# The first two stages of a bidirectional Mamba loop: convolution on VectorE, token tiles ahead of the loop, a new slot table

## What is computed

```
x   = patches @ W_tok.T                              # 16 tiles of 98 tokens
xz  = layernorm(x) @ W_in.T ; xc, z = split(xz)      # 384 + 384 channels
xconv = silu(conv_b + sum(conv_w[:, k] * xc[t + k - 3] for k in range(4)))
proj  = xconv @ W_x.T ; dtr, B, C = split(proj)      # 12, 16, 16
dt  = softplus(dtr @ W_dt.T + b_dt)
h[t] = exp(dt * A) * h[t-1] + (dt * xconv) * B       # 16 states per channel
y   = (sum_n h * C + xconv * D) * silu(z)
out += y @ W_out.T
```

## Time and profile before

| | us |
|---|---|
| median of three runs | 1530.7 |
| profiled execution, time / span | 1525.57 / 1523.8 |
| TensorE busy | 1337.1 (88%) |
| VectorE busy | 911.9 (60%) |
| ScalarE busy | 672.0 (44%) |
| GpSimd busy | 553.1 (36%) |
| granted TensorE clock, mean | 0.949 |

### The profile page before, as it was taken

How to read it: one execution, slowest core, us unless ns; L and a number is a source line. 1 busy time by engine, 2 the same in 40 slices (tenths; PEclk the granted TensorE clock), 3 DMA queues, 4 the chain that set the end, 5 groups by cost and what they waited for, 6 DMA issues and landing times.

```text
span 1523.8 us, 18483 instructions
## 1 busy us (share of the span) xinstructions
PE 1337.1 (88%) x6708; PEld 774.0 (51%) x6708; DVE 911.9 (60%) x1501; ACT 672.0 (44%) x1209; POOL 553.1 (36%) x399
## 2 busy tenths in 40 slices
PE   7888898898989877649988859989999899999998
PEld 6644454454545434326443345547856659445444
DVE  2487999999999999983100038865546624221122
ACT  4656777676767754232110106641542241313311
POOL 1266798989798887500000020012025302000000
PEclk9999899999999999869999969999999999999999
DMA  6504040504133240062999950000010000020101
GB/s 203 170 2 143 27 143 28 169 13 160 52 120 97 74 160 10 28 283 95 396 400 392 400 148 1 1 0 1 1 37 2 2 1 15 23 100 22 37 1 32
DMA packets 38773, 151.96 MB, mean 100 GB/s; under 512 B 10364, under 2 KB 14587, under 8 KB 33948
## 3 DMA queue, kind: packets, MB, share of 16 engines
q1 hardware_dynamic: 34588, 149.21, 27.7%
q10 hardware_dynamic: 4096, 1.58, 0.4%
HBM read 147.56 MB, written 1.63 MB: 98 GB/s over the span
## 4 chain that ended last, share of the span: by engine, by line
PE 54%; DVE 20%; issue 10%; ACT 6%; DMA 5%; POOL 3%; SPq 1%; ACTq 0%; DVEq 0%; POOLq 0%
PE ps L1854 53%; DVE arena L1452 7%; DVE arena L1441 4%; DMA arena<-in_e_b 4%; POOL arena L822 3%; ACT arena L924 2%; ACT ps L1035 1%; DVE stats L1372 1%; PE ps L1863 1%; DVE arena L1737 1%; ACT arena L929 1%; DVE arena L1461 1%; SPq L634 1%; DVE arena L1492 0%; DVE arena L1741 0%
## 5 line engine op out<-in xcount | busy, mean ns | idle before, releaser
L1854 PE MATMUL ps<-arena 128*98 128x192 f32 (+14 forms) x5260 | 954.7, 416 | 100.7 <-DVE arena L1502 25.1
L1854 PEld LDWEIGHTS ps<-arena 128*98 128x98 f32 (+12 forms) x5260 | 543.6, 154 | 483.3 <-issue 285.5
L822 POOL TENSOR_TENSOR arena<-arena 128x784 f32<-128x784 f32 x192 | 367.6, 1928 | 109.0 <-DVE arena L1452 108.4
L1854 PE MATMUL ps<-arena,ident 128*128 128x392 f32 x900 | 353.3, 523 | 48.4 <-POOL arena L822 40.2
L1452 DVE TENSOR_TENSOR_SCAN arena<-ps,arena 128x784 f32<-128x784 f32 x192 | 341.7, 1780 | 9.5 <-ACT ps L1035 9.5
L1854 PEld LDWEIGHTS ps<-arena,ident 128*128 128x128 f32 x900 | 172.0, 198 | 197.7 <-POOL arena L822 68.9
L924 ACT ACTIVATE arena<-ps 128x392 f32<-128x392 f32 (+9 forms) x265 | 124.3, 487 | 302.7 <-PE ps L1854 218.2
L1035 ACT ACTIVATE ps<-arena 128x384 f32<-128x384 f32 x384 | 207.8, 574 | 106.8 <-DVE arena L1452 106.2
L924 ACT ACTIVATE arena<-ps,arena 128x392 f32<-128x392 f32 (+2 forms) x194 | 105.1, 601 | 231.5 <-PE ps L1854 146.4
L1441 DVE TENSOR_TENSOR arena<-ps,arena 128x784 f32<-128x784 f32 x192 | 183.4, 956 | 12.6 <-issue 6.9
L1600 DVE COPY arena<-ps 128x384 f32<-128x384 f32 x32 | 16.4, 553 | 150.7 <-PE ps L2103 150.7
(11 more groups left out here) (199 smaller groups left out, 856.3 us busy)
## 6 DMA issues: line engine op xcount, KB each, us to landing
arena<-in_e_w SPq DMA_DIRECT2D x32, 2304.0 KB
arena<-bc_rows SPq DMA_DIRECT2D x128, 392.0 KB, 4.7
arena<-in_patches SPq DMA_DIRECT2D x4, 1176.0 KB, 7.7
arena<-comb_rows SPq DMA_DIRECT2D x1, 3136.0 KB, 10.7
arena<-in_mlp_w SPq DMA_DIRECT2D x5, 576.0 KB, 4.4
arena<-arena ACTq DMA_DIRECT2D x128, 12.0 KB, 8.5
arena<-in_mlp_w SPq DMA_DIRECT2D x5, 384.0 KB, 3.7
arena<-in_mlp_w SPq DMA_DIRECT2D x10, 192.0 KB, 4.0
```

Of the source, the lines that this page charges most:

```text
L822: pool.tensor_tensor(pair(hbuf[:, at % SLOTS, :]), pair(hbuf[:, at % SLOTS, :]), c_all[:, n:n + 2, :], ALU.mult).then_inc(times_c, 1)
L1854: return pe.matmul(dst, lhsT, rhs, start=first, stop=last)
```

## The change

The first stage's convolution leaves TensorE and its copies leave ScalarE: VectorE does it from the padded `xc` with one scale-and-bias and three multiply-adds per block (`first_conv`), interleaved with the silu products; the norm of tiles 4 to 7 moves behind them. `first_products` now counts nine steps, looked up by name in `FIRST_DONE`. All 16 token tiles use banks 0 to 5, are copied out ahead of the loop, and tiles 8 to 10 stand ahead of the first projection on TensorE. The second stage's preparation gets new slots: inner products in -3 to -1 (were 0 to 2), convolutions in 0 to 2 (were 4, 6, 8), projection 7 (11), steps 9 to 10 (12 to 13), du 20 (22); its z products take the usual slots. The third stage loses its exceptions. The late norm moves from slot 8 to 12 and its scalings from 10 to 14.

```diff
@@ -68,23 +68,22 @@
 EARLY = {
-    0: {"z_pe": (25, 26, 27), "z_act": (27, 28, 29), "tanh_z_act": (30, 31), "silu_z_pool": (31, )},
-    1: {"xc_pe": (0, 1, 2), "xc_act": (2, 3, 4), "conv_pe": (4, 6, 8), "conv_act": (6, 8, 9), "tanh_act": (9, 10),
-        "silu_pool": (10, ), "proj_pe": (11, ), "proj_act": (12, ), "step_pe": (12, 12, 13), "step_act": (13, 13, 14),
-        "exp_act": (15, ), "ln_act": (16, ), "inverse_act": (17, ), "s_pool": (17, ), "square_act": (19, 20, 21),
-        "series_dve": (20, 21), "dt_pool": (21, ), "du_pool": (22, ), "z_pe": (13, 17, 22), "z_act": (15, 19, 25)},
-    2: {"xc_pe": (-10, -9, -8), "xc_act": (-7, -6, -5), "conv_pe": (-6, -4, -2), "conv_act": (-4, -2, 0)}}
-TOK_LATE = 3 * TQ
-TOK_ACT = {0: (12, 13), 1: (14, 15)}
+    0: {"z_pe": (26, 27, 28), "z_act": (28, 29, 29), "tanh_z_act": (30, 31), "silu_z_pool": (31, )},
+    1: {"xc_pe": (-3, -2, -1), "xc_act": (0, 0, 1), "conv_pe": (0, 1, 2), "conv_act": (2, 3, 4), "tanh_act": (4, 5),
+        "silu_pool": (5, ), "proj_pe": (7, ), "proj_act": (9, ), "step_pe": (9, 9, 10), "step_act": (11, 11, 12),
+        "exp_act": (12, ), "ln_act": (13, ), "inverse_act": (14, ), "s_pool": (14, ), "square_act": (16, 17, 18),
+        "series_dve": (17, 18), "dt_pool": (18, ), "du_pool": (20, )}}
+FIRST_DONE = {name: i + 1 for i, name in enumerate(
+    ("conv0", "conv1", "x0", "conv2", "x1", "x2", "s", "dt", "du"))}
 REST_SQUARE, REST_SERIES, REST_POOL = 2, 3, 3
-NORM_DVE, NORM_ACT = 8, 10
+NORM_DVE, NORM_ACT = 12, 14
 WKV = ((0, 0), (0, 1), (1, 0), (1, 1), (0, 2), (0, 3))
...
 LATE_TURN_PE, LATE_TURN_ACT = (5, 25, 48), (7, 28, 50)
-SCHEDULE = range(-1, LOOPED + 14)
+SCHEDULE = range(-3, LOOPED + 14)
 TIMES = {}
@@ -377,12 +376,12 @@
         s_tok, s_xhT = stage("tok", "act"), stage("transp", "act")
-        for i in range(TOK_LATE):
+        for i in range(NT):
             use(s_tok, [i % 6], "act")
...
         side = 0
-        for s, n in ((s_xhT, 2), (s_xc, 3), (s_cv, 3), (s_xp, 1), (s_st, 3), (s_tok, NT - TOK_LATE)):
+        for s, n in ((s_xhT, 2), (s_xc, 3), (s_xp, 1), (s_st, 3)):
             for i in range(n):
@@ -825,7 +824,7 @@
                     pool.wait_ge(dt_ready, 1)
-                    pool.wait_ge(first_products, 3)
+                    pool.wait_ge(first_products, FIRST_DONE["x2"])
                     pool.tensor_tensor(du[:, 0, 1:3], dt[:, 0, 1:3], xconv[:, 0, 1:3], ALU.mult).then_inc(du_ready, 1)
@@ -961,7 +960,7 @@
 
-                i = 3 * s + c
+                i = 3 * (s - 1) + c
                 copy_out(s_cv, i, xconv[:, s % 2, c, :], bank(s_cv.banks[i][0], 128, 0, QT),
@@ -993,26 +992,26 @@
             for c in range(3):
-                conv_out(0, c)
-                s_cv.wait_taken(act, c)
+                act.wait_ge(first_products, FIRST_DONE[f"conv{c}"])
                 own.then(act.activation(g_t[:, c], xconv[:, 0, c], ACT.Tanh, scale=0.5))
...
                     .then_inc(tanh_ready, 1)
-            token_out(8)
+            for i in (8, 9):
+                token_out(i)
             proj_out(0)
...
             own.then(act.activation(e_t, e_t, ACT.Exp, scale=-1.0))
-            act.wait_ge(first_products, 3)
+            act.wait_ge(first_products, FIRST_DONE["x2"])
             own.then(act.activation(g_t, e_t, ACT.Ln, bias=act_c[:, 0:1]))
...
             act.activation(g_t[:, 1:3], g_t[:, 1:3], ACT.Exp, scale=-1.0).then_inc(r_ready, 1)
-            act.wait_ge(first_products, 4)
+            act.wait_ge(first_products, FIRST_DONE["s"])
             series_squares(slice(0, 1), 0)
-            for i in range(9, TOK_LATE):
+            for i in range(10, NT):
                 token_out(i)
-            s_tok.wait_taken(act, TOK_LATE - 1)
+            s_tok.wait_taken(act, NT - 1)
 
@@ -1022,7 +1021,7 @@
                 else:
-                    act.wait_ge(first_products, 5)
+                    act.wait_ge(first_products, FIRST_DONE["dt"])
                 act.wait_ge(aneg_ready, 2)
@@ -1041,8 +1040,6 @@
                     decay(at)
-                for i in TOK_ACT.get(at, ()):
-                    token_out(i)
                 if at == REST_SQUARE:
@@ -1057,7 +1054,7 @@
                         else:
-                            act.wait_ge(first_products, 6)
+                            act.wait_ge(first_products, FIRST_DONE["du"])
                         if s + c > 0:
@@ -1065,8 +1062,10 @@
                     if s is not None:
-                        if s > 0:
-                            s_cv.wait_filled(act, 3 * (s - 1) + c)
+                        if s > 1:
+                            s_cv.wait_filled(act, 3 * (s - 2) + c)
+                        else:
+                            act.wait_ge(first_products, FIRST_DONE[f"conv{c}"])
                         xc_out(s, c)
@@ -1075,7 +1074,7 @@
                 if s is not None:
-                    s_cv.wait_taken(act, 3 * s + 2)
+                    s_cv.wait_taken(act, 3 * (s - 1) + 2)
                     act.wait_ge(l_ready, s)
@@ -1404,13 +1403,36 @@
             dve.nop().then_inc(xc_edges, 1)
-            for k in range(2):
+            def tokens_normed(k):
+
                 norm_stats(h, range(TQ * k, TQ * k + TQ), lambda i: s_tok.wait_taken(dve, i))
...
                     normalise(xh, h, i, rstd).then_inc(xh_ready, 1)
-            for c in range(3):
+
+            def first_conv(c):
+
+                s_xc.wait_taken(dve, c)
+                to = steps_of(xconv[:, 0, c, :])
+                own.then(TS(to, xc[:, c, :, 0:TOKENS], taps[0][:, c, 0:1], conv_b[0][:, c:c + 1], ALU.mult, ALU.add))
+                for k in range(1, TAPS):
+                    ins = STT(to, xc[:, c, :, k:k + TOKENS], taps[0][:, c, k:k + 1], to, ALU.mult, ALU.add)
+                    if k < TAPS - 1:
+                        own.then(ins)
+                ins.then_inc(first_products, 1)
+
+            def first_silu(c):
+
                 dve.wait_ge(tanh_ready, c + 1)
                 TT(xconv[:, 0, c], xconv[:, 0, c], g_t[:, c], ALU.mult).then_inc(first_products, 1)
+
+            tokens_normed(0)
+            first_conv(0)
+            first_conv(1)
+            first_silu(0)
+            first_conv(2)
+            first_silu(1)
+            first_silu(2)
+            tokens_normed(1)
 
@@ -1423,10 +1445,10 @@
             TT(dt[:, 0, 0], dt[:, 0, 0], relu_t[:, 0], ALU.add).then_inc(first_products, 1)
-            dve.wait_ge(first_products, 5)
+            dve.wait_ge(first_products, FIRST_DONE["dt"])
             TT(du[:, 0, 0], dt[:, 0, 0], xconv[:, 0, 0], ALU.mult).then_inc(first_products, 1)
             s_xhT.wait_taken(dve, 1)
-            s_tok.wait_filled(dve, TOK_LATE - 1)
+            s_tok.wait_filled(dve, NT - 1)
 
@@ -1921,7 +1943,7 @@
                     if s == 0 and c == 0:
-                        s_tok.wait_taken(pe, TOK_LATE - 1)
+                        s_tok.wait_taken(pe, NT - 1)
                     pe.wait_ge(diag_ready, (2, 4)[s % 2])
@@ -1933,9 +1955,9 @@
 
-                i = 3 * s + c
+                i = 3 * (s - 1) + c
                 pe.wait_ge(diag_ready, (1, 3)[s % 2])
-                s_xc.wait_taken(pe, i)
+                s_xc.wait_taken(pe, 3 * s + c)
                 s_cv.fill(pe, i)
@@ -1968,15 +1990,14 @@
                 inner(s_xc, c, 128 * c, 0)
-            pe.wait_ge(xc_edges, 1)
-            for c in range(3):
-                convolved(0, c)
-            token(8)
-            projected(0, lambda c: pe.wait_ge(first_products, c + 1))
+            for i in range(8, 11):
+                token(i)
+            projected(0, lambda c: pe.wait_ge(first_products, FIRST_DONE[f"x{c}"]))
             for c in range(3):
                 stepped(0, c)
-            for i in range(9, NT):
+            for i in range(11, NT):
                 token(i)
+            pe.wait_ge(xc_edges, 1)
             for at in SCHEDULE:
```

## The result

The changed kernel takes 1514.7 us (median of four runs, 1509.0 to 1516.4) against 1530.0 for the kernel before (1528.3 to 1532.5, four runs): a ratio of 0.9892, 95% interval 0.9863 to 0.9922, so about 1% less time. The profiled execution has a time of 1509.02 and a span of 1507.3 us, 16.5 under the span of before.

The account below looks back on a forecast made before the run. VectorE bounds the loop; the prologue's chain and the first stage's 20.0 us idle were open. Prologue 3.5 and stage 15.4 gave 18.9, less 0.2 for waits: 18.7 off 1530.7, 1512.0 us, range 1505 to 1521.

Parts of the forecast that it names:

- The convolution: Prologue: VectorE takes 2.44 per channel block, last silu ends 38.8, projection's copy starts 39.75 against 43.26, 3.5 us earlier.
- The loop's start: Ahead of the loop: first product at 55.7 against 59.24, with tiles 11 to 15 on TensorE from 43.3 to 53.4.
- the cover of 1.3 us: End of the prologue: ScalarE is through the tile copies at 53.8, du's copy can start at 55.1.
- Slots 0 to 12: First stage: stalls of 1.0 at decay 5, 2.2 at decay 6, 0.9 at du's copy, 0.7 at decay 12.
- The norm and behind it: Slots 12 to 14: norm of tiles 8 to 15 costs the same 6.3 on VectorE; scalings and inverse cost 1.2.
- The stage's end: Slots 17 to 20: GpSimd's C products delay du; product 24 at 134.8, VectorE ready at 133.9, wait 0.9.
- The port: Prologue: VectorE and GpSimd exclude each other, nine added multiply-adds exposed; takes nothing off the sum, as GpSimd has nothing there.
- A: Rival, slots 0 to 7 or gate in slot 9: heavy slots cost 3 to 10 more, 1519; chance 0.14.
- B: Rival, slots 18 to 20: du still late on GpSimd, 3 to 6 of 6.9 remains, 1516 to 1518; chance 0.11.
- C: Rival, first stage: nearly all stalls go, the 6 us left in the forecast vanish, 1506; chance 0.07.
- D: Rival, prologue: multiply-adds at 1.24 leave it no gain, even with half of that, 1515.5; chance 0.03.
- E: Rival, slots 0 to 6: TensorE at 1.2 GHz, its string takes 24 us more, slower at 1533; chance 0.04.

Follow-up runs that it names:

- the two executions with the short drop: Changed kernel with the late norm's scalings in slot 20, and changed kernel with the second stage's du in slot 19: medians 1512.1 and 1514.9 us.
- fillers: Changed kernel plus useless 128x128 transposes on TensorE, four ahead of the first two steps and four ahead of the third: median 1515.9 us.

## Why the prediction was right, and where not
The median came at 1514.7 against 1512.0 forecast and inside the range of 1505 to 1521; the spans differ by 16.5 where I had 18.7. The forecast's own mechanism held; two terms of the sum were mis-sized to the bad (the loop's start and the scalings), one to the good (the norm).

- **The convolution.** Right. A channel block took 2.40 (2.44 forecast: the multiply-adds start 0.66 apart, not 0.61, the scale-and-bias was cheaper, 0.48), the last silu ended at 38.63 (38.8) and the projection's copy started at 39.59 (39.75). That the norm moved behind it costs nothing was right too: it ended at 44.2, and VectorE then stood for 6.6 us.
- **The loop's start.** Wrong by 1.6: 55.7 forecast, 57.27 measured. The step that failed is "tiles 11 to 15 follow the steps on TensorE, 43.3 to 53.4 (five of 2.02)", on which the cover of 1.3 us rested. It took the clock of the earlier trace rows for granted; with TensorE at 1.2 GHz until 48.7 the tiles ended at about 56.2, ate the cover and 1.0 more, and the third step was 0.7 late. In the two executions with the short drop the forecast was right within 0.3.
- **Slots 0 to 12.** Right, stall by stall. Decay 5: 0 (I had it absorbed by the series); decay 6: 1.96 (2.2); du's copy: 0.64 (0.9); decay 12: 0.54 (0.7). The second multiply-add of the series took 2.50 as before. The copy of the projection held no decay.
- **The norm and behind it.** Half right. "It costs the same on VectorE" was wrong by 1.0 in my favour: 5.4 us from the first operation to the next product, not 6.3, as the operation that had met a GpSimd product met none. Product 16 waited 2.44 where I had 1.2, and I had nothing for the gate of slot 17, which waited 0.92. The step that failed is that the scalings and the inverse "push decay 15 and du's third copy: 1.2": ScalarE's order also has the copy of a z product and, before them, decay 14 behind a table load, and TensorE, whose bank waits for that copy, stood 6.8 us and came back at 1.2 GHz. The runs with the scalings in slots 20 or 19 to 22 show the scalings to be the cause of the first wait. The second needs the slow TensorE behind them and came in three of the five profiles that had the pause of 6.8 us and the changed kernel's convolution and tiles; for it the cause is shown in part.
- **The stage's end.** Right: 1.03 (0.9), and the cause named for it, GpSimd's queue, is shown by the run with du in slot 19. Of the 12.4 us that the table gave, this is the part that the old slots bring back whole (6.9 against 1.0).
- **The port.** The rule of the Trainium skill (SBUF — State Buffer, section "Who interferes with whom") that I weighed was without effect ahead of the loop, as I had it: GpSimd was idle from 25.4 to 43.0, over the whole convolution. It shows once more in the after trace, with VectorE first this time: the series' multiply-add kept its 1.36 and GpSimd's product took 2.91 instead of 1.85:

```profile
125.06 1.36 DVE L1518 SCALAR_TENSOR_TENSOR arena<-arena 128x1176 f32<-128x1176 f32 x1
...
125.22 2.91 POOL L821 TENSOR_TENSOR arena<-arena 128x784 f32<-128x784 f32 x1 [2.43 <-DVE arena L1474]
```

- **The rivals.** A's heavy slots cost about what the forecast gave them (3.1 us in slots 5 to 12, 3.8 forecast); B's late du left 1.0 of 6.9; C and D didn't come. E, the lower clock in slots 0 to 6, didn't come: the clock was 1.00 from 55.8 to 100 (and 0.95 before). It fell ahead of the loop instead, where I had not expected it, and behind the norm.
- **From span to median.** I carried the gain over the 5.1 us between the profiled execution and the median as if they were fixed. They aren't: the code behind the last scan, the same in all kernels, took 894.6 to 905.9 us in thirteen profiles. Both first profiles lie at its low end, by chance, so the spans' 16.5 is a clean difference, and the medians' 15.3 has this spread in it. The 1370 us that the prediction counts "from the loop's end on" run from product 24: they were 1369.6 in the first profile of the changed kernel and 1379.5 in the second, so that sign holds only as far as this spread allows.

## What to carry to other kernels
When engines keep a fixed order, a stage is won by giving the preparation of the next one more distance, but only as far as the engine that makes it is free: here 12.4 of 16 us came from the slot table. The table needs the token tiles out of the loop (with four of them in it the stage took 88.4, not 80.4), and the tiles ahead of the loop cost 4 us there until the convolution leaves TensorE, which gives 6 back; the table itself did as well with the convolution on TensorE (80.1). String the busiest helper engine's work together with its banks and compare it with the units that it must meet; this gave each stall within 0.3 us up to the norm. Every copy that TensorE waits for belongs in the string; the one behind the scalings was missing from the forecast. And test a saving at a place behind the next meeting point of the engines (a product far down), not where it is made: 1.2 us at the first product were 0.1 six units later.

## What the runs showed of the hardware
The granted clock of TensorE fell to half for 3 to 7 us around the projection and the steps in all eleven profiles of the new order, with a length that differed for the same code (44 to 47 and 42 to 48.7), and it fell as well where fillers kept the engine busy for 2.00 of 2.00 us ahead of it. The Trainium skill (TensorE: Matmul & The Clock Gate, section "HAM oscillation — how this bites in real kernels") lays such drops to idle gaps between matmuls. The drop at 106.7, inside the 6.8 us without a matmul behind the norm, agrees with it, the one with fillers doesn't; there the measurement decides, and its cause is open.

The second thing is the spread of unchanged code. Two profiles of the same kernel, 1507.3 and 1517.4 us long, part behind the last scan. TensorE there in the first and in the second:

```profile
1300.00:1310.00 10.00, 10.00 (x36) 1.00 0.00 1
...
1320.00:1330.00 10.00, 6.39 (x22) 0.83 0.32 115
1330.00:1340.00 10.00, 10.00 (x43) 1.00 0.49 208
```

```profile
1300.00:1310.00 10.00, 10.00 (x22) 0.75 0.00 0
...
1320.00:1330.00 10.00, 9.66 (x48) 0.73 0.01 2
1330.00:1340.00 10.00, 6.73 (x13) 0.66 0.40 143
```

The low stretches between 1295 and 1355 us add up to 3.4 us in the first and 20.6 in the second; half of the difference, 8.6, is my estimate of what they cost. Comparing the same instructions, the second profile fell 7.2 us further behind there, and had fallen 2.9 behind before, most of it from 740 to 1010 us. A change of a few us in this kernel can only be judged by marks ahead of that place.
